# Attention body: three steps re-ordered on VectorE; last channel tile: a probability and a copy on other engines

## The reference, cut to what matters

```
x = x + tanh(g_xattn[0]) * channel_attention(layernorm(x), ctx)   # per batch item: R = q k, softmax, attention @ v
x = x + tanh(g_ffn[0])   * clustered_linear(layernorm(x))
x = x + tanh(g_xattn[1]) * attention(layernorm(x), ctx, ctx, mask) # 32 query heads, 8 key/value heads, rotary embedding
x = x + tanh(g_ffn[1])   * quantised_swiglu(layernorm(x))
...
q = rope(query @ wq); k = rope(key @ wk); v = value @ wv
attn = softmax(q k^T / sqrt(128) + mask);  out = (attn @ v) @ wo
rope(t) = t * cos + rotate_half(t) * sin
```

## Time and profile before

| | |
|---|---|
| time, median of 3 runs | 802.04 us (801.54 to 805.16) |
| time of the profiled execution | 802.02 us, of which 800.2 us are its span |
| PE busy | 760.5 us (95% of the span) |
| DVE busy | 639.9 us (80%) |
| POOL busy | 388.5 us (49%) |
| ACT busy | 352.1 us (44%) |

### The profile page before, as it was taken

One profiled execution on the slowest core, in us unless ns is written; L12 is line 12 of the kernel. 1 busy time (PEld: TensorE's weight loads), 2 busy tenths in 40 slices (PEclk: granted clock), 3 DMA queues, 4 the chain that ended last, 5 costly groups with the idle time before them and its releaser, 6 DMA issues.

```text
span 800.2 us, 12768 instructions
## 1 busy us (share of the span) xinstructions
PE 760.5 (95%) x4278; PEld 606.7 (76%) x4278; DVE 639.9 (80%) x1209; ACT 352.1 (44%) x1077; POOL 388.5 (49%) x352
## 2 busy tenths in 40 slices
PE   3999998998989999999999999999999999999996
PEld 2666674986768788888877888887788888787875
DVE  5999997879887887777788777777877678768984
ACT  4788785312333434333343433334243433344664
POOL 2888895423552533324253332335333333386784
PEclk9999999998999999999999999999999999999998
DMA  7221240110110201111020101101110112200011
GB/s 244 56 64 39 74 123 2 40 53 0 53 53 28 67 27 40 32 35 40 27 66 28 40 27 40 40 28 53 39 42 27 29 39 79 59 27 1 2 40 67
DMA packets 38087, 37.45 MB, mean 47 GB/s; under 512 B 3024, under 2 KB 27344, under 8 KB 38032
## 3 DMA queue, kind: packets, MB, share of 16 engines
q1 hardware_dynamic: 37168, 36.48, 15.5%
q10 hardware_dynamic: 864, 0.27, 0.2%
HBM read 34.64 MB, written 2.10 MB: 46 GB/s over the span
## 4 chain that ended last, share of the span: by engine, by line
PE 62%; DVE 8%; POOL 5%; issue 2%; ACT 1%; POOLq 0%; DVEq 0%; ACTq 0%
PE ROW L2090 7%; PE QB L2092 6%; PE QB L2090 6%; PE SB L2205 6%; PE QB L2091 6%; PE ROW L2091 6%; PE ROW L2092 6%; PE PB L2178 4%; DVE rope_b L1705 2%; PE KV L729 2%; PE KV L2090 2%; PE TB L2148 2%; PE KV L2092 2%; PE KV L2091 1%; PE KV L730 1%
## 5 line engine op out<-in xcount | busy, mean ns | idle before, releaser
L1270 POOL TENSOR_TENSOR dense<-rope_a,rope_b 128x512 f32<-128x512 f32 x62 | 79.2, 1277 | 163.7 <-DVE rope_b L1705 163.7
L1484 ACT ACTIVATE ot_hi<-PB 128x512 fp32r<-128x512 f32 x64 | 38.3, 598 | 199.2 <-PE PB L2178 199.1
L1473 ACT ACTIVATE e_sb<-masked,nmax 128x64 f32<-128x64 f32 x256 | 86.1, 337 | 57.0 <-DVE nmax L1736 56.7
L2090 PE MATMUL QB<-xT_hi,wq_lo 128*128 128x512 f32 x256 | 106.9, 418 | 0.0
L2090 PE MATMUL ROW<-wo_hi,ot_lo 128*128 128x512 f32 x256 | 102.1, 399 | 0.8 <-DVE ot_lo L1764 0.8
L1702 DVE TENSOR_TENSOR rope_a<-QB,rope 128x512 f32<-128x512 f32 x62 | 42.8, 691 | 74.0 <-PE QB L2092 72.0
L2092 PE MATMUL QB<-xT_hi,wq_hi 128*128 128x512 f32 x256 | 101.7, 397 | 0.0
L2091 PE MATMUL ROW<-wo_lo,ot_hi 128*128 128x512 f32 x256 | 101.6, 397 | 0.0
L2091 PE MATMUL QB<-xT_lo,wq_hi 128*128 128x512 f32 x256 | 101.6, 397 | 0.0
L2092 PE MATMUL ROW<-wo_hi,ot_hi 128*128 128x512 f32 x256 | 101.1, 395 | 0.0
L1705 DVE TENSOR_TENSOR rope_b<-QB,rope 64x512 f32<-64x512 f32 x124 | 85.3, 688 | 3.9
(11 more groups left out here) (215 smaller groups left out, 1880.2 us busy)
## 6 DMA issues: line engine op xcount, KB each, us to landing
raw<-in_wq SPq DMA_DIRECT2D x32, 256.0 KB, 2.7
raw<-in_wo SPq DMA_DIRECT2D x32, 256.0 KB, 2.6
ctx_two<-in_ctx SPq DMA_DIRECT2D x16, 256.0 KB, 3.9
x_sb<-in_x SPq DMA_DIRECT2D x8, 256.0 KB, 5.9
ctx_raw<-in_ctxT SPq DMA_DIRECT2D x8, 256.0 KB, 3.9
raw<-in_wv SPq DMA_DIRECT2D x8, 256.0 KB, 2.7
raw<-in_wk SPq DMA_DIRECT2D x8, 256.0 KB, 3.0
out<-x_sb SPq DMA_DIRECT2D x8, 256.0 KB, 2.1
```

The lines of the kernel that those rows point to most:

```text
L1270: nc.gpsimd.tensor_tensor(dst, a, b, ALU.add).then_inc(s_rot, 1)
L1473: nc.scalar.activation(e_sb[:, r, :], masked[:, r, :], ACT.Exp, bias=nmax[:, r:r + 1], accum_out=zsum[:, r:r + 1]).then_inc(s_exp, 1)
L1484: nc.scalar.activation(ot_hi[:, :, :].rearrange("p h (b q) -> p b h q", b=2), PB2[:, :, 0:256].rearrange("p b (h q) -> p b h q", h=GH), AC ...
L2090: nc.tensor.matmul(out, lhs[1], rhs[0], start=first, stop=False)
```

## The change: what it does

In the last channel tile, the product `prob * rz` of block 6 is done by DVE (`last_probabilities`, with a semaphore of its own, `s_plast`) where POOL did it, and the copy of block 7 out of `TP[1]` is done by ACT where DVE did it. `inverse(7, 7)` is ahead of `value(7)`, and POOL no longer waits for its own last product ahead of `ctx_lo`.

In the attention block, `rest_x(6)` is one place later, behind the rope of query h = 3. The rope of the second key (`KV`, half 1 of `k_rot`) comes ahead of all ropes of the body, in two parts around `mask_and_max(0)`; it was in step 1. In steps 0 to 2 the mask and maximum come ahead of the ropes and a step's normalisation ahead of the next query's rope. `q_job` and POOL's order of `rotate` follow.

```diff
@@ channel_attention, ACT @@
-                                     TP[0][:, :].rearrange("p (j t) -> p j t", j=KC),
+                                     TP[u % 2][:, :].rearrange("p (j t) -> p j t", j=KC),
...
             for i in range(6, 8):
                 step(i)
+            evacuate(TILES - 1, 7)
@@ channel_attention, DVE @@
+            def last_probabilities():
+                dve.wait_ge(s_rz, 8 * TILES - 1)
+                nc.vector.tensor_tensor(prob[:, 2, :], prob[:, 2, :], rz[:, 6:7].broadcast_to([P, D]),
+                                        ALU.mult).then_inc(s_plast, 1)
...
             inverse(7, 6)
+            last_probabilities()
+            inverse(7, 7)
             value(7)
-            inverse(7, 7)
             evacuate(7, 5)
...
             variance_eps(nc, c, s_var2, 0, TILES - 1)
-            evacuate(7, 7)
@@ channel_attention, POOL @@
-                if outside(t):
+                if outside(t) or isinstance(t, int) and (t, u) == (TILES - 1, 6):
                     return
@@ attention, job numbers @@
-    return JOBS * gp + 5 + n + sum(s < n for s in K_SLOTS) - (n <= K_SLOTS[-1] - SLOTS)
+    return JOBS * gp + 5 + n + sum(s < n for s in K_SLOTS) - (n <= K_SLOTS[-1] - SLOTS) + (gp == 0 and n in (0, 1))
+FIRST_K = 5
@@ attention, POOL @@
+                    if N == 0:
+                        rotate(FIRST_K, k_dst(1))
@@ attention, DVE @@
-                rest_x(4 + h)
+                if h != 2:
+                    rest_x(4 + h - (h == 3))
...
+            rest_x(7)
             rest_v(0, 7, FIRST_V[7])
+            rope_first_key(0)
+            mask_and_max(0, 0)
+            rope_first_key(1)
+            normalize(0)
+            mask_and_max(1, 1)
+            rest_pt(0)
+            rope_q(q_job(0, 0), 4, 0)
+            normalize(1)
+            rest_ot(0)
+            mask_and_max(2, 2)
+            rest_pt(1)
+            rope_q(q_job(0, 1), 5, 1)
+            normalize(2)
+            rope_q(q_job(0, 2), 6, 2)
+            accumulate(0, 0)
+            rest_ot(1)
...
-                for n in range(SLOTS):
+                for n in range(0 if gp else 3, SLOTS):
```

More of the change, by code:

```diff
@@ L130, in channel_attention @@
         s_w, s_whi, s_wlo = sem("w_loaded"), sem("w_hi_ready"), sem("w_lo_ready")
-        s_lxn = sem("first_xn_ready")
+        s_lxn, s_plast = sem("first_xn_ready"), sem("last_prob_by_dve")
         s_var2, s_rstd2 = sem("new_var_ready"), sem("new_rstd_ready")
@@ L537, in waited @@
             def waited(t, s, n):
-                if not outside(t):
+                if not outside(t) and not (isinstance(t, int) and t == TILES - 1 and n == 8 * TILES):
                     pool.wait_ge(s, n)
@@ L657, in transposes @@
                     return
-                pe.wait_ge(s_p, 8 * t + u + 1)
+                if isinstance(t, int) and t == TILES - 1 and u >= 6:
+                    if u == 6:
+                        pe.wait_ge(s_plast, 1)
+                    else:
+                        pe.wait_ge(s_p, 8 * TILES - 1)
+                else:
+                    pe.wait_ge(s_p, 8 * t + u + 1)
                 if later(t) or u >= 2:
@@ L670, in outputs @@
                     return
-                pe.wait_ge(pt_act, 4 * t + 4)
-                pe.wait_ge(pt_dve, 4 * t + 4)
+                moved = isinstance(t, int) and t == TILES - 1
+                pe.wait_ge(pt_act, 4 * t + 4 + moved)
+                pe.wait_ge(pt_dve, 4 * t + 4 - moved)
                 pe.wait_ge(s_vsb, t + 1)
@@ L1293, in pair @@
                 for n in range(SLOTS):
+                    N = SLOTS * gp + n
+                    if N == 0:
+                        rotate(FIRST_K, k_dst(1))
                     if n < 12 or ahead:
                         rotate(q_job(gp, n), q_dst(n // 4 + 1, n % 4))
-                    if n in K_SLOTS and (n != 13 or ahead):
+                    if n in K_SLOTS and N != 1 and (n != 13 or ahead):
                         rotate(q_job(gp, n) + 1, k_dst((K_SLOTS.index(n) + 1) % 2))
@@ L1693, in _, with rope_parts @@
         def _(dve):
-            def rope_parts(job, src, is_k, places, last_read):
+            def rope_parts(job, src, is_k, places, last_read, part=None):
                 cos = rope[:, 2 * is_k, :].unsqueeze(1)
@@ L1701, in rope_parts @@
                     dve.wait_ge(s_rot, last_read)
-                nc.vector.tensor_tensor(a, v, cos.broadcast_to([P, 8, S]), ALU.mult).then_inc(s_parts, 1)
+                if part != 1:
+                    nc.vector.tensor_tensor(a, v, cos.broadcast_to([P, 8, S]), ALU.mult).then_inc(s_parts, 1)
                 for h in range(2):
+                    if part == 1 - h:
+                        continue
                     rows, other = slice(S * h, S * h + S), slice(S * (1 - h), S * (1 - h) + S)
@@ L1714, in rope_k, with rope_first_key @@
                 rope_parts(job, KV, 1, parts, job)
+            def rope_first_key(part):
+                dve.wait_ge(s_k, 2)
+                rope_parts(FIRST_K, KV, 1, parts, FIRST_K, part)
             def rope_first(job, produced, n, src, is_k):
@@ L1828, in _ @@
                     rope_first(q_job(0, h - GH) + 1, s_k, 1, KV, 1)
+            rest_x(7)
             rest_v(0, 7, FIRST_V[7])
+            rope_first_key(0)
[14 more added lines that the diff above has]
+            rest_ot(1)
             def pair(gp, ahead):
-                for n in range(SLOTS):
+                for n in range(0 if gp else 3, SLOTS):
                     N = SLOTS * gp + n
                     mask_and_max(N, n % 8)
[L1835 to L1838, removed]
+                    rest_pt(N - 1)
                     if n < 12 or ahead:
                         rope_q(q_job(gp, n), N + 4, n % 4)
-                    if N:
-                        normalize(N)
+                    normalize(N)
                     if N >= 2:
```

## The result

The changed kernel took 797.91 us (median of 5 runs, 797.06 to 799.03) against 802.36 us (5 runs, 801.54 to 805.16) of the kernel before: a ratio of 0.9942, interval 0.9927 to 0.9957. The medians differ by 4.45 us, the ratio stands for 4.65 (3.4 to 5.9). Run again beside other kernels, it took 796.48 against 802.09: 0.9931 (0.9917 to 0.9944), by the ratio 5.5 us less. The forecast was 796.9, with 795.8 to 799.2 as its range. That range also holds the rivals (a), (b) and (c), at 798.5, 798.2 and 798.8, and 797.91 is not nearer to the forecast than to (a) or (b): which of them happened is told by the profile, not by the time.

The account below looks back on a forecast made before the run. PE, busy 95% of the span, was taken as the bound, so only its waits and low clock pay. Terms 0.7 + 0.6 + 2.2 + 1.6 = 5.1 us, off 802.0, gave 796.9, range 795.8 to 799.2.

Parts of the forecast that it names:

- (a): Body: the clock falls all the same, in one stretch like the old one, +1.6 us, 798.5; chance 0.11.
- (b): Step 0: POOL's waiting key rotation goes ahead of DVE's waiting p_sb, which ends 1.27 later; 798.2, chance 0.08.
- (c): Step 1's gap survives as rope_q(0) awaits the key's rotation, or later DVE steps run short; 798.8, worst 801; chance 0.10.
- Term 1: Last channel tile: ACT's copy of block 7 follows its transposes at once, so the outputs start earlier; -0.7 us.
- Term 2: Body start: moving rest_x(6) lets query 3's rope and POOL's rotation come earlier, so score(0) starts sooner; -0.6 us.
- Term 3: Step 1: one rope, not two, between the products of steps 0 and 1, so transposes(1) start earlier; -2.2 us.
- Term 4: Behind transposes(1): the clock stays at 1.00, without the 1.2 GHz stretch up to the outputs; -1.6 us.
- (d): Attention body: the edit doesn't help and only terms 1 and 2 hold; 800.7 us, chance 0.04.
- (e): Body: PE's idle stretches lie closer together and bring 1.2 GHz up to outputs(1); slower, some 805 us; chance 0.05.

Follow-up runs that it names:

- e7: Kernel before with only block 7's last copy moved to ACT, block 6's product left on POOL: one run, 802.39 us (before 802.09).
- e6: Changed kernel with rest_x(6) back in its old place ahead of the rope of query 3: 797.15 us for 802.94, ratio 0.9931.
- e3: Kernel before with only step 1's normalisation moved ahead of query 1's rope, the key's rope staying in step 1: 803.63 us for 802.51, ratio 1.0017.
- e5: Changed kernel with query 1's rope back ahead of step 1's normalisation, the key's rope staying early: 802.57 us for 802.94, ratio 0.9997.
- e4: Kernel before with eight unused PE products filling the gap ahead of transposes(1): 801.76 us for 802.51, ratio 0.9992.
- e1: Kernel before with only the last channel tile's changes, attention block as before: 801.28 us for 802.51, ratio 0.9985.
- e9: e8 with POOL's rotation of the key ahead of all four wo_lo: 802.34 us for 802.94, ratio 0.9990.
- e2: Kernel before with only the attention block's changes, last channel tile as before: 797.63 us for 802.51, ratio 0.9943.
- e8: Changed kernel with DVE's copy of block 5 ahead of the values and two value rests behind the key's rope: 796.56 us for 802.94, ratio 0.9921.
- e10: e8 with POOL's rotation of the key behind the second of the four wo_lo: 795.18 us for 802.09, ratio 0.9915.

## Why the prediction was right, point by point

- **The sum.** 5.1 was forecast; 4.65 and 5.5 us were measured in total (by the ratios), 5.09 by the anchors. All four terms hold within 0.05 us. The total alone could not have told this: the first timing is 1.0 above the forecast and 0.3 from rival (b), and it moves by more than that with the first load and the clock near the start.
- **Term 1, 0.7.** 0.72. That the transposes of block 7 would gain nothing was nearly right: the product on DVE moves them by 0.07 (e7), which is what the forecast's own times, 131.90 for 131.97, say.
- **Term 2, 0.6.** 0.59, and 0.58 when undone alone (e6). The wait ahead of score(0) is 0.87, in the forecast 0.8 to 0.9.
- **Term 3, 2.2.** transposes(1) come 2.83 earlier, 2.24 of it beyond term 2. The idle time is 0.22 where I had 0.4, by a slip in the sum: transposes(0) at 216.46, then 3.17 + 0.55, then 1.10 for score(2), make 221.28 and not 221.1. The reason was right too, with one addition: e3 shows that the new order alone only moves the gap, e5 that the key's early rope alone leaves it, and e6, with both, has 0.22 of idle time.
- **Term 4, 1.6.** The stretch behind transposes(1) is 1.56 shorter. As a price of the low clock by itself the figure is too high: e4 gives 0.9. The sum was right since the other terms put DVE ahead at the same time. In part it was luck: the profile of before had the short low stretch. Behind waits of 2.0 to 3.8 us it was 3.4 us long in three profiles (before, e5, e7) and 6.8 in three (e1, e3, e9), and with the long one as the start the term would have been about 1 us larger.
- **The rivals.** (a), a low clock all the same, didn't come in the two profiles of after, nor in e2, e6, e8 and e10; its price was sound for a short low stretch. The argument against it was weaker than I made it: e1 shows the clock falling behind an idle time of 1.40. (b), POOL's waiting rotation first, did not happen: the product took 1.01 us and the rotation came behind it. The row at 20.34, on which (b) rested, was misread: DVE waited there for one instruction of POOL, not two (last section), and the same profile has seven meetings in which the waiting DVE went first. (c) did not happen: `rope_a` of query 0 starts at 218.78, 0.13 behind the end of the key's rotation and without a wait (the forecast had 0.2 to spare), transposes(1) wait 0.22, and the largest wait of PE in steps 2 to 4 is 0.23, ahead of score(4), as before. (d) is refuted by e2, and (e) by the windows at 1.00.
- **What the forecast lacked.** Nothing in its sum; but e5 and e9 show two waits near the path that it had priced by "each us there is one lost" alone: POOL's rotation between two ropes through one pair of buffers, and the transfer that a `wo_lo` sets free. Neither binds in the kernel after.

## What to carry to other kernels

Where an engine is late at one step, look for its idle time ahead of the steps and move work there: an exchange inside the step pushes the gap on (e3), the move alone leaves it (e5), and the two together remove it. Price a gap on PE as gap plus the low clock behind it only if the engine it waits for is early afterwards; with that engine still late, just over half of the clock's part was had (0.88 of 1.56). And take that price from more than one profile: the same code showed it with low stretches of 3.4 and 6.8 us. Before reordering splits of arriving weights, follow the buffer that each frees to the transfer it starts and to what stands behind that in the queue: a rotation put ahead of four splits cost 5.8 us, put behind the second of them it gained 0.5 by the anchors.

## What the runs showed of the hardware that was not expected

- The clock's answer to a gap is not the same in each execution: an idle time of 1.40 us ahead of score(0) was followed by 0.50 in e1 and by 1.00 at 1.42 in before. Every low stretch between 18 and 250 us in the profiles here, near 20 us, near 185 and in the body, was 3.4 or 6.8 us long, and the same code showed both: near 20 us 6.8 in one profile of the kernel after and 3.4 in the other. What decides between them is not shown.
- DVE and POOL, both waiting while the other works: a DVE product issued 0.73 us before the end of a POOL instruction went ahead of POOL's next one, which took 1.47 for 1.28. This is the common case. The earlier trace rows shows two `ctx_stk` products of POOL in one row; taken singly, the first runs from 19.05 to 20.31, and the second is the first line here. The other two are one more meeting in the profile of before:

```profile
20.39 1.27 POOL L533 TENSOR_TENSOR ctx_stk<-ctx_two,ctx_stk 64x512 fp32r<-64x512 f32 x1
...
43.87 0.88 DVE L310 TENSOR_SCALAR xn<-x_sb,mv,rstd 128x512 f32<-128x512 f32 x1
...
44.42 1.23 POOL L562 TENSOR_TENSOR prob<-prob,rz 128x512 f32<-128x512 f32 x1
```

The DVE instruction at 20.34 came 0.03 us behind the end of POOL's first one and waited for the second alone, whose record starts 0.05 us later; it ended 0.28 us behind it. At 43.87 DVE waited 0.59 us for a POOL product, went ahead of POOL's next one, and that took 1.23 for 1.04. The profile of before has seven such meetings of DVE's normalisations and products with a queued POOL, the one of after ten, with waits of 0.4 to 1.1 us: DVE went first in each, and no profile here has one in which it waited for two. What is open is only who goes first when both come within some hundredths of a microsecond.
